# Fold blocks of a cross-attention kernel: three a group instead of four, the bias with the first

## What is computed

```python
qh = (q @ Wq + bq).reshape(Bn, Tq, H, DK)
kh = (k @ Wk + bk).reshape(Bn, Tk, H, DK)
vh = (v @ Wv + bv).reshape(Bn, Tk, H, DK)
attn = jnp.einsum('bqhd,bkhd->hbqk', qh, kh) * mask[None]
attn = attn - jnp.max(attn)
attn = jnp.exp(attn) * mask[None]
attn = attn / (jnp.sum(attn, axis=-1, keepdims=True) + 1e-15)
out = jnp.einsum('hbqk,bkhd->bqhd', attn, vh).reshape(Bn, Tq, H * DK) @ Wo + bo
x = out + residual      # then layer norm over the last axis, times gamma, plus beta
```

## Time and profile before

| | us |
|---|---|
| median of 3 runs | 1605.37 (1605.35 to 1605.41) |
| the profiled execution | 1605.02 |
| its span | 1603.2 |

### The profile page before, as it was taken

How to read it: one execution, slowest core, us unless ns; L and a number is a source line. 1 busy time by engine, 2 the same in 40 slices (tenths; PEclk the granted TensorE clock), 3 DMA queues, 4 the chain that set the end, 5 groups by cost and what they waited for, 6 DMA issues and landing times. The chain is left out here.

```text
span 1603.2 us, 31952 instructions
## 1 busy us (share of the span) xinstructions
PE 1587.2 (99%) x11142; PEld 772.0 (48%) x11142; DVE 1167.8 (73%) x2399; ACT 885.6 (55%) x1357; POOL 582.2 (36%) x876
## 2 busy tenths in 40 slices
PE   8999999999999999999999999999999999999998
PEld 4555455455554555555544444444444444444444
DVE  7767475765575756656655998888888888888885
ACT  6555454554554545545445666666666666666652
POOL 0000000000000000000000498888888888888875
PEclk9999999999999999999999999999999999999999
DMA  6584575562844656638455866556655566655522
GB/s 230 191 272 146 165 218 178 174 215 97 271 146 152 211 178 177 212 103 279 139 161 171 325 263 262 218 220 244 255 205 220 219 252 262 242 216 222 210 80 79
DMA packets 100469, 323.80 MB, mean 202 GB/s; under 512 B 10128, under 2 KB 14352, under 8 KB 90640
## 3 DMA queue, kind: packets, MB, share of 16 engines
q1 hardware_dynamic: 100368, 322.32, 57.7%
HBM read 192.26 MB, written 130.02 MB: 201 GB/s over the span
## 5 line engine op out<-in xcount | busy, mean ns | idle before, releaser
L110 PE MATMUL ps_s<-x_hi,g_hi 128*128 128x512 f16 x1024 | 388.7, 380 | 0.8 <-issue 0.3
L119 PE MATMUL ps_o<-u,p_hi 128*128 128x512 f16 (+1 forms) x1024 | 387.9, 379 | 0.2 <-DVE p_lo L1363 0.2
L112 PE MATMUL ps_s<-x_hi,g_lo 128*128 128x512 f16 x1024 | 388.1, 379 | 0.0
L111 PE MATMUL ps_s<-x_lo,g_hi 128*128 128x512 f16 x1024 | 388.1, 379 | 0.0
L120 PE MATMUL ps_o<-u,p_hi 128*128 128x512 f16 (+1 forms) x1024 | 387.2, 378 | 0.0
L121 PE MATMUL ps_o<-u,p_lo 128*128 128x512 f16 (+1 forms) x1024 | 387.2, 378 | 0.0
L637 ACT ACTIVATE s<-ps_s,c_bias 128x512 f32<-128x512 f32 x256 | 176.5, 689 | 354.8 <-PE ps_s L112 352.6
L872 POOL PARTITION_ALL_REDUCE key_max<-early_max x1 | 0.7, 712 | 852.9 <-DVE early_max L794 852.9
L1197 ACT ACTIVATE p_hi<-ps_bc 128x512 f16<-128x512 f32 x256 | 152.2, 596 | 160.4 <-DVE ps_bc L1357 160.4
L785 DVE TENSOR_TENSOR score_max<-score_max,tile_max 128x1 f32<-128x1 f32 x257 | 40.6, 158 | 269.9 <-ACT s L637 267.7
L1516 POOL TENSOR_TENSOR y<-y,gamma_b 128x512 f32<-128x512 f32 x124 | 157.7, 1272 | 86.1 <-ACT y L1218 86.1
(11 more groups left out here) (140 smaller groups left out, 2460.3 us busy)
## 6 DMA issues: line engine op xcount, KB each, us to landing
scores<-s SPq DMA_DIRECT2D x30, 2048.0 KB, 7.6
x<-xT_in SPq DMA_DIRECT2D x32, 1024.0 KB, 10.2
u_halves<-u_out SPq DMA_DIRECT2D x256, 128.0 KB, 2.9
u<-u_halves SPq DMA_DIRECT2D x16, 2048.0 KB, 11.5
s_more<-scores SPq DMA_DIRECT2D x16, 2048.0 KB, 9.6
y<-x_in SPq DMA_DIRECT2D x32, 1024.0 KB, 7.6
out<-y SPq DMA_DIRECT2D x31, 1024.0 KB, 5.0
s<-scores SPq DMA_DIRECT2D x14, 2048.0 KB, 9.4
```

The source lines that it names most:

```text
L110: pe.matmul(out, lhs_hi, rhs_hi, start=first, stop=False)
L111: pe.matmul(out, lhs_hi, rhs_lo, start=False, stop=False)
L112: return pe.matmul(out, lhs_lo, rhs_hi, start=False, stop=last)
L119: pe.matmul(out, lhs_hi, rhs_hi, start=False, stop=False, skip_group_check=True)
```

## The change

The keys' folds of a group's boundary go in three blocks (`BLOCKS`): pairs 0 and 1 behind tile 3 of the last unit, as before; pairs 2, 3 and 4 behind tile 6; pairs 5, 6 and 7 ahead of tile 1 of the next group's first unit. The third pair of a block uses the two banks `ps_k` (`key_bank`), which are free of the bias by then. The bias follows the first block instead of the second. The waits of `fold_q` for free banks shrink to one for each block, for all tiles up to the block before it; the second block also waits for `c_ready`, since the bias' banks are used by it. ScalarE waits before pair 2 for two more score tiles than before pair 0, since pair 4's values are read by later tiles. Group 0's own folds stay as they were.

```diff
+        BLOCKS = ((0, 1), (2, 3, 4), (5, 6, 7))
+
+        def key_bank(first, p, h):
+
+            if first:
+                return ps_f[(2 * p + h) % GBANKS]
+            of = next(block for block in BLOCKS if p in block)
+            return (ps_f + ps_k)[2 * of.index(p) + h]
+
         def late_folds(first):
-            return {1: (2, 3), 2: (4, 5), 4: (6, 7)} if first else {1: (4, 5), 3: (6, 7)}
-
-
-        early_folds = {3: (0, 1), 5: (2, 3)}
+            return {1: (2, 3), 2: (4, 5), 4: (6, 7)} if first else {1: BLOCKS[2]}
+
+
+        early_folds = {3: BLOCKS[0], 6: BLOCKS[1]}
...
-                pe.wait_ge(f_lo_done, g * FT + 2 * p + 2)
-                tiles = [ps_f[(2 * p + h) % GBANKS] for h in range(2)]
+
+                if first:
+                    pe.wait_ge(f_lo_done, g * FT + 2 * p + 2)
+                elif p in (0, 2, 5):
+                    pe.wait_ge(f_lo_done, g * FT + 2 * p + GBANKS)
+                    if p == 2:
+                        pe.wait_ge(c_ready, 2 * g + 1)
+                tiles = [key_bank(first, p, h) for h in range(2)]
...
-                        if p == max(early_folds):
+                        if p == min(early_folds):
                             bias(g + 1)
...
-            def round_g(g, p):
-                if p == 0 and not (isinstance(g, int) and g == 0):
-
-                    act.wait_ge(s_summed, (g * UNITS + 1) * NP + EARLY)
+            def round_g(g, p, first):
+                if p in (0, 2) and not first:
+
+                    act.wait_ge(s_summed, (g * UNITS + 1) * NP + (EARLY if p == 0 else EARLY + 2))
...
-                    act.activation(of_folded(g_hi, p, h), by_key_halves(ps_f[i % GBANKS]),
+                    act.activation(of_folded(g_hi, p, h), by_key_halves(key_bank(first, p, h)),
...
-                    dve.scalar_tensor_tensor(of_folded(g_lo, p, h), by_key_halves(ps_f[i % GBANKS]),
+                    dve.scalar_tensor_tensor(of_folded(g_lo, p, h), by_key_halves(key_bank(first, p, h)),
...
-                        if p == max(early_folds):
+                        if p == min(early_folds):
                             bias(g + 1)
```

More of the change, by code:

```diff
@@ L634, in scores_out @@
                         for pair in late_folds(first).get(1 if first and p == 0 else 0 if first and p == 1 else p, ()):
-                            round_g(g, pair)
+                            round_g(g, pair, first)
                     act.wait_ge(s_summed, n * NP + p + 1 + 2 * NP)
@@ L648, in scores_out @@
                         for pair in early_folds[p]:
-                            round_g(g + 1, pair)
+                            round_g(g + 1, pair, False)
                     if p == NP // 2 and not (last and u == UNITS - 1):
@@ L686, in _ @@
             round_x(0, 0)
-            round_g(0, 0)
-            round_g(0, 1)
+            round_g(0, 0, True)
+            round_g(0, 1, True)
             split_weight(5)
@@ L727, in split_kv, with split_g @@
                                          ALU.mult, ALU.subtract).then_inc(kv_lo_done, 1)
-            def split_g(g, p):
+            def split_g(g, p, first):
                 for h in range(2):
@@ L801, in mask_scores @@
                         for pair in late_folds(first).get(p + 1, ()):
-                            split_g(g, pair)
+                            split_g(g, pair, first)
                         if p == 0:
@@ L825, in mask_scores @@
                         for pair in early_folds[p]:
-                            split_g(g + 1, pair)
-                        if p == max(early_folds):
+                            split_g(g + 1, pair, False)
+                        if p == min(early_folds):
                             bias(g + 1)
@@ L852, in _ @@
             split_x(0, 0)
-            split_g(0, 0)
-            split_g(0, 1)
+            split_g(0, 0, True)
+            split_g(0, 1, True)
             split_weight(5)
```

## The result

The changed kernel takes **1608.5 us**, the median of 21 runs (1607.55 to 1610.27). The kernel before, on the same chip, takes 1605.39 us (21 runs, 1604.49 to 1605.94). The ratio is 1.002, with a 95% interval of 1.0014 to 1.0025. That is a small loss, 3.1 us by the medians, and it lies right at the bound of 0.2% that the prediction had drawn. The predicted time was 1608.3, in a range of 1606.3 to 1610.1.

The account below looks back on a forecast made before the run. TensorE, busy for 99% of the span at full clock, was taken as the bound. Profiled 1605.02 - 1.5 (fewer blocks) + 4.4 (jumps) = 1607.9; with the runs' median 0.35 above the profiled one, 1608.3, range 1606.3 to 1610.1.

Parts of the forecast that it names:

- the bound of 0.2%: Limit of what a measurement can tell from no change: 3.2 us, that is 1602.2 and 1608.6.
- The mechanism: At TensorE's five loop jumps, one score tile instead of two covers the branch; each gap is its length less 2.49 us.
- the step on which it all hung: On TensorE's sequencer, the loop's branch starts about 0.25 us before the pass's last score tile, covering 2.84 us.
- issue: Profile label expected for TensorE gaps of 0.8 to 1.4 us ahead of the first score matmul of passes two to six.
- Fewer blocks: Three fold blocks instead of four at each of seven group boundaries save 0.22 us each, -1.5 us.
- Jumps: Five jumps back of TensorE's loop lose 5.1 us instead of 0.71, +4.4 us; bounds +3.4 and +6.3.
- Bias: Moved to the first block, its matmuls change nothing on TensorE and VectorE's twelve small operations end in time; cost nothing.
- Waits at the third block: At p = 5 TensorE waits for all splits of the second block; 2.0 us of slack on VectorE, cost nothing.
- The jump stays hidden: Rival at TensorE's loop jump: only the saved switches count, 1603.9 us; chance 0.12.
- VectorE late: Rival at the third block: VectorE's splits start 2.9 us later and TensorE waits, 1610.1 us; chance 0.06.
- No saving of switches: Rival in the fold blocks: a third pair costs half a block, 0.78 us, so 1609.8 us; chance 0.05.
- all branches short, all long: Five jumps all at 3.308 us give 1607.3, all at 3.884 give 1610.2; the range was taken as 1606.3 to 1610.1.

Follow-up runs that it names:

- experiments 1 and 2: TensorE's loop written out: changed kernel 1603.3 us, kernel before 1604.77; second block one tile forward in changed kernel 1604.24, one tile back in kernel before 1610.25.
- experiment 6: Changed kernel with work left out to shorten TensorE's loop from 1848 instructions a pass: 1595.15 us with 1592 instructions, 1524.78 with 1336.
- the two written-out kernels: Changed kernel and kernel before, each with TensorE's loop over groups 1 to 6 written out, so nothing jumps: 1603.3 us and 1604.77.
- experiment 3: Kernel before with only the bias moved behind the first block instead of the second: 1605.25 us, ratio 1.0.
- experiment 4: Changed kernel with TensorE's loop written out and its third block one score tile sooner: 1607.77 us, 4.6 above the written-out kernel.
- experiment 7: Changed kernel with group 0's bias matmuls issued three times, putting 128 instructions ahead of the unchanged loop: 1610.17 us, ratio 1.0046 to the kernel before.
- experiment 5: Changed kernel with its second block behind tile 7 instead of tile 6, directly ahead of the jump: 1636.12 us, ratio 1.0197 to the kernel before.
- the shortened kernel: Changed kernel whose keys' folds after group 0 keep one of three terms, 1592 instructions a pass on TensorE: 1595.15 us, one run.

## Why the prediction was right

**The mechanism** was the one predicted: the jump back loses cover because one score tile stands behind the last block instead of two. The four runs that take away the jump, undo the place, or make the change of place alone agree (experiments 1 and 2), and the step on which it all hung, the branch 0.25 us ahead of the pass's last tile, was read at other places of the trace and came out so: 237.88 against 238.13. What the branch waits for, a piece of code, is seen in the packets of all five jumps (experiment 6). One sign was off: the prediction said that the profile would call the gaps "issue", and it puts them down to ScalarE's copy and VectorE's splits.

**The sum, term by term.** Fewer blocks: -1.5 predicted, -1.47 between the two written-out kernels. Jumps: +4.4 predicted, 5.48 - 0.71 = +4.8 in the profiled execution. Here the working was right and the lengths were a little off: the branches summed to 17.91 us instead of the 17.54 taken over from before, and that is the difference. The prediction had given this its own small chance. Bias: nothing, and nothing (experiment 3). Waits at the third block: nothing, with 1.9 us of slack instead of 2.0 (experiment 4). The terms give +3.3; between the first and the last score matmul the two traces differ by 3.3 (845.86 and 849.18 us). The profiled executions are 3.75 apart, since in the changed kernel's the first scores began 0.35 later, ahead of any block that was changed; the medians are 3.1 apart.

**The rivals.** *The jump stays hidden* (1603.9): refuted, five of five jumps show it. With the jumps gone the changed kernel takes 1603.3, so that is indeed what the jumps keep from it. *VectorE late* (1610.1): it isn't late; it is with the block one tile sooner. *No saving of switches* (1609.8): refuted by the 2.22 of the block and by the 1.47.

**What was weak, and what was luck.** The prediction had no price of its own for a branch, only the five that the trace showed, and it took their sum for its forecast. That sum changes from one execution and one kernel to the next: 17.4 to 18.3 us in seven traces. The changed kernel's runs span 2.7 us. So that the median lies within 0.2 of the forecast is in part luck. For the profiled execution the sum gave 1607.9, and it took 1608.77: 0.4 more by the branches, 0.35 by the later start. In experiment 7 the same loop at another place has branches of 19.9 us (one trace; the medians of the two kernels lie 1.9 apart, each against its own kernel before). The change itself alters the code ahead of the loop. Had it come out like experiment 7, 5.0 above the kernel before, the time would have been 1610.4, over the range. The bounds of the range (all branches short, all long) weren't bounds either: its upper end was cut at 1610.1 while the long ones gave 1610.2, and the longest branch that before's trace showed (3.884) was passed by the changed kernel's first (3.907) and by all but one of the moved loop's.

## What to carry to other kernels

Where TensorE is the bound, look at its sequencer's branches as well as at its matmuls: a jump back costs only what lies beyond the work already queued, so the last thing before the jump should be a long stretch of wide matmuls, not small ones. Saving instructions by moving them nearer to the jump can lose more than it saves; here 1.5 us were gained and 4.8 lost, and the version that keeps the gain without a jump beats both. A gap that the profile puts down to an engine that had long been done is a reason to look at the sequencer, and then at the packets of the instruction queue around its branch.

## What the runs showed of the hardware

- The price of a jump back of TensorE's loop does not grow evenly with the loop: 0.21 us with 1336 instructions a pass, 3.3 to 4.0 with 1592 to 1850, and up to 4.17 for the same loop moved by 128 instructions.
- What it waits for is a piece of code of 16 KB: the branch ends 1.30 to 1.48 us after that packet's landing, in 40 of 40 long jumps; 15 short ones have no packet.
- A gap can cost once more behind it. After 3.2 us nearly idle the granted clock was 0.56 over the next 3.8 us, and the first tile took 1.6 us more (experiment 5, four of five jumps; the fifth, after 3.03 us, not); after 1.6 us it stayed at 1.00.
- Behind a long jump TensorE can run dry a second time, where the fetched piece ends: 12 instructions on in the shortened kernel, 110 on in experiment 5, for 0.8 to 2.9 us, each time until 1.2 to 1.6 us after the next piece had landed. In experiment 5 that piece was asked for 4.4 to 4.7 us after the branch's end, instead of 0.6 to 1.3; why is not shown. The changed kernel comes to the same place late enough.
- Going into row-tiled matmuls and out again costs 0.21 us a block, with two pairs in it or three: 0.22 read from one block, 0.21 from 1.47 us over seven.
